# Two-layer gated attention: modulation rows computed in row form, first unit and last tiles reordered, and the second layer's norm bias folded in on GpSimd

## What is computed

```python
xn = _ln(x, ln_w, ln_b)
q = softmax(heads(xn @ Wq + bq), axis=channels of a head)
k = softmax(heads(xn @ Wk + bk + mask), axis=tokens)
v = (xn @ Wv + bv) * mask
att = einsum('bnhd,bnhl->bhdl', k, v)
y = einsum('bnhd,bhdl->bnhl', q, att)
scale, shift = split(silu(emb) @ W_emb + b_emb, 2)      # "film": one pair of rows for each sequence
hh = _ln(y, ln2_w, ln2_b) * (1.0 + scale) + shift
return x + silu(hh) @ W_out + b_out
```

## Time and profile before

| | |
|---|---|
| median of 3 runs | 791.82 us |
| lowest and highest | 791.3 and 793.96 us |
| the profiled execution's own time | 790.92 us |
| its span (first to last instruction) | 789.1 us |
| busy share PE, DVE, ACT, POOL | 96%, 88%, 66%, 56% |
| mean granted TensorE clock | 0.996 of full speed |
| chain of work that ended last | PE 78%, DVE 12%, ACT 4% |

### The profile page before, as it was taken

How to read it: one execution, slowest core, us unless ns; L and a number is a source line. 1 busy time by engine, 2 the same in 40 slices (tenths; PEclk the granted TensorE clock), 3 DMA queues, 4 the chain that set the end, 5 groups by cost and what they waited for, 6 DMA issues and landing times.

```text
span 789.1 us, 17594 instructions
## 1 busy us (share of the span) xinstructions
PE 760.7 (96%) x6719; PEld 405.7 (51%) x6719; DVE 693.9 (88%) x1427; ACT 517.4 (66%) x1011; POOL 439.3 (56%) x433
## 2 busy tenths in 40 slices
PE   5997999999999999999999999999999999999996
PEld 2446446464564545546464554646464554645442
DVE  7898979788998999999988899898888899888985
ACT  5896767666667687786866685665658476560733
POOL 2465583653836768487664755547265535637323
PEclk9998999999999999999999999999999999999999
DMA  9966896865949759596585939688594939578452
GB/s 325 311 132 168 271 183 192 161 145 150 185 139 161 189 129 182 170 173 189 109 188 138 195 108 184 165 161 201 93 203 120 187 122 178 130 140 156 83 132 81
DMA packets 291252, 130.78 MB, mean 166 GB/s; under 512 B 261440, under 2 KB 261824, under 8 KB 291168
## 3 DMA queue, kind: packets, MB, share of 16 engines
q1 hardware_dynamic: 288432, 125.27, 71.1%
q10 hardware_dynamic: 2736, 4.39, 1.6%
HBM read 47.74 MB, written 16.88 MB: 82 GB/s over the span
## 4 chain that ended last, share of the span: by engine, by line
PE 78%; DVE 12%; ACT 4%; issue 3%; DMA 2%; SPq 1%; POOL 0%; DVEq 0%; ACTq 0%; POOLq 0%
PE ring L534 59%; PE ring L583 5%; PE ring L589 3%; PE att_ps L682 3%; DVE sb_k_or_qt L1069 2%; PE ring L730 2%; PE ring L594 2%; DMA sb_k_or_qt<-sb_tanh 1%; ACT sb_k_or_qt L1467 1%; PE ring L738 1%; DVE sb_row_peak L908 1%; DVE sb_q_max L1102 1%; DVE ring L1099 1%; DVE sb_ht_parts L1185 1%; DVE ring L1104 1%
## 5 line engine op out<-in xcount | busy, mean ns | idle before, releaser
L534 PE MATMUL ring<-sb_w_hi,sb_xt_parts 128*128 128x512 f16 x1024 | 309.2, 379 | 0.0
L534 PE MATMUL ring<-sb_w_lo,sb_xt_parts 128*128 128x512 f16 x512 | 194.2, 379 | 0.0
L534 PEld LDWEIGHTS ring<-sb_w_hi,sb_xt_parts 128*128 128x128 f16 x1024 | 100.4, 98 | 126.0 <-issue 6.6
L534 PE MATMUL ring<-sb_w_hi,sb_ht_parts 128*128 128x512 f16 x512 | 155.9, 380 | 4.3 <-DVE sb_ht_parts L1303 1.4
L1725 POOL TENSOR_TENSOR sb_htok<-sb_ht_parts,sb_htok 128x512 f16<-128x512 f32 x60 | 75.0, 1271 | 127.8 <-ACT sb_htok L1500 127.8
L1741 POOL TENSOR_TENSOR sb_tanh<-sb_v_or_q,sb_kq_hi 128x512 f16<-128x512 f32 x64 | 74.0, 1157 | 87.6 <-ACT sb_kq_hi L1531 87.0
L534 PE MATMUL ring<-sb_w_lo,sb_ht_parts 128*128 128x512 f16 x256 | 97.1, 379 | 0.0
L1524 ACT ACTIVATE sb_v_or_q<-ring,sb_ln_one 128x512 f32<-128x512 f32 x64 | 43.9, 686 | 60.9 <-DVE ring L1104 60.8
L534 PEld LDWEIGHTS ring<-sb_w_hi,sb_ht_parts 128*128 128x128 f16 x512 | 50.1, 98 | 63.7 <-ACT sb_ht_parts L1637 4.1
L1716 POOL TENSOR_TENSOR sb_x<-sb_x,sb_bias_o 128x512 f32<-128x512 f32 x64 | 79.3, 1276 | 5.8 <-DVE sb_w_lo L985 5.8
L534 PEld LDWEIGHTS ring<-sb_w_lo,sb_xt_parts 128*128 128x128 f16 x512 | 50.1, 98 | 59.4 <-issue 0.7
(11 more groups left out here) (244 smaller groups left out, 1573.5 us busy)
## 6 DMA issues: line engine op xcount, KB each, us to landing
out<-sb_x SPq DMA_DIRECT2D x14, 1024.0 KB, 5.8
sb_rows_now<-film_rows SPq DMA_DIRECT2D x16, 512.0 KB, 4.8
sb_x<-out SPq DMA_DIRECT2D x8, 1024.0 KB, 5.3
sb_x<-in_x SPq DMA_DIRECT2D x7, 1024.0 KB, 5.5
sb_mask_add<-mask_terms SPq DMA_DIRECT2D x15, 256.0 KB, 6.1
sb_w_hi<-in_L_cond_W_emb SPq DMA_DIRECT2D x1, 1536.0 KB, 14.0
sb_w_lo<-in_L_cond_W_emb SPq DMA_DIRECT2D x1, 1536.0 KB, 14.3
sb_w_hi<-in_L_cond_film_emb_W ACTq DMA_DIRECT2D x1, 1536.0 KB, 11.7
```

What stands on the lines that cost most here:

```text
L534: last = nc.tensor.matmul(out, lhs, rhs, start=(n == 0), stop=(n == len(pairs) - 1))
```

## The change

- Film stays in rows. Channel groups of 128 lie in four groups of 32 partitions; b_emb comes in by matmuls; `turn_film`, `turn_table` and four ACT copies go. The second norm's weight and bias are turned into rows once at the start (`ln2_in_rows`, one ACT copy). The rows are stored by four DMAs in place of two, in unit 0 between two transposes of the SP queue.
- Unit 0: film products come after query tiles 0 and 2; DVE does `v_scales` ahead of query tile 2, mixes values with queries, and does `mask_attention` ahead of most sums; attention uses half-width matmuls; x sums and squares of unit 2 move behind. The output weight's peak goes to the end of unit 0 on DVE, its scale and split into unit 1: on ACT ahead of `high_values(1)`, on POOL ahead of `low_values(1)`, its sum on PE after value tile 0. Both halves of layer 1's film weight are loaded by ACT in unit 1.
- Units 3 to 5: `shift_parts` and its ACT copy go; POOL does it with four multiplications and three additions of 128x512 float32, between `low_x` and `low_h`, once the weight is loaded.
- Unit 15: ACT takes the scaled values out of PSUM in float32 and then as float16; POOL makes the low part, so that DVE has no values to do.
- Tail: ACT's Silu replaces tanh and DVE's gate; h's power of two goes into the split; transposes on PE go in between matmuls of the projections.

```diff
@@ sync @@
             def store_table(layer):
-                sp.wait_ge(table_copied, 2 * (layer + 1))
-                for n in range(2):
-                    sp.dma_start(film_d[layer, :, n, :], table[film_part[n], :]).then_inc(film_stored, 16)
+                sp.wait_ge(film_ready, layer + 1)
+                for c in range(C):
...
+                    sp.dma_start(out, film[rows:rows + B].rearrange("b n (j e) -> b n j e", j=2)).then_inc(film_stored, 16)
...
-                turn_x(0, 1)
+                turn_x(0, 1, (0,))
+                store_table(0)
+                turn_x(0, 1, (1,))
@@ tensor @@
             def film_product(layer, half):
...
+                for c in range(C):
+                    at = B_EMB + C * half + c
+                    nc.tensor.matmul(out[film_part[c], :], cols[:, layer, at:at + 1].broadcast_to([P, 32]), ident[:], start=True, stop=False)
                 for k in range(KE):
-                    g = slice(k % 4 * 32, k % 4 * 32 + 32)
-                    last = nc.tensor.matmul(film_at(half)[g, :], emb_wide[:, k, :], film_w_at(half, k), start=(k < 4), stop=(k >= 4))
+                    for c in range(C):
+                        last = nc.tensor.matmul(out[film_part[c], :], emb_wide[:, k, :], film_w_at(half, k)[:, c * P:c * P + P],
+                                                start=False, stop=(k == KE - 1))
                 last.then_inc(film_half, 1)
...
             def shift_sums(layer, m):
-                pe.wait_ge(shift_copied, folded(layer, m))
+                if layer:
+                    pe.wait_ge(shift_row, 4 * PREPARED[1].index(m) + 4)
+                else:
+                    pe.wait_ge(shift_copied, folded(layer, m))
...
-                project_tokens("V", 0, V_, xt_hi, xt_lo, between=with_v)
-                first_attention(between=lambda: turn_table(0))
-                pe.wait_ge(table_copied, 2)
-                sum_w(0, O_)
+                project_tokens("V", 0, V_, xt_hi, xt_lo)
+                bound_film(0)
+                first_attention()
                 attend(0)
...
-                    if shifted is not None and i == 0:
+                    if shifted is not None and i == 2:
                         pe.wait_ge(h_ready, 4 * u)
-                        shift_parts(1, shifted)
-                    elif shifted is not None and i == 2:
                         shift_sums(1, shifted)
...
+                def with_v(i):
+                    if u == 1 and i == 0:
+                        sum_w(0, O_)
...
-                output(u - 1, (2, 3))
+                output(u - 1, (2,))
+                output(u - 1, (3,), at=((2, lambda: turn_h(0)),))
...
-            turn_h(0)
             turn_h(1)
             last_output(0)
-            last_output(1)
-            turn_h(2)
-            last_output(2)
-            turn_h(3)
+            last_output(1, ((1, lambda: turn_h(2)),))
+            last_output(2, ((2, lambda: turn_h(3)),))
             last_output(3)
@@ vector @@
+            def rows_of_film(layer):
...
+                for n in range(2):
+                    link(nc.vector.scalar_tensor_tensor(out=film[:, n, :], in0=film_at(0), scalar=1.0, in1=ln2_rows[:, layer, n, :],
+                                                        op0=ALU.add, op1=ALU.mult))
+                link(nc.vector.tensor_tensor(film[:, 1, :], film_at(1), film[:, 1, :], ALU.add))
...
             def keys_beside_h(u):
...
+                if u == 1:
+                    find_scale(0, O_)
+                    output_scale(0)
...
                 queries(0, 1)
+                v_scales(0)
                 queries(0, 2)
+                values(0, 0)
                 queries(0, 3)
-                v_scales(0)
-                values(0, 0)
                 values(0, 1)
                 values(0, 2)
-                gather_film(0)
+                rows_of_film(0)
                 values(0, 3)
+                find_film_peak(0)
+                query_sums(0, (0,))
                 film_scales(0)
-                find_peak(0, O_)
-                query_sums(0)
-                query_recip(0)
                 dve.wait_ge(blocks_loaded, 16)
                 mask_attention(0)
-                find_scale(0, O_)
-                output_scale(0)
+                query_sums(0, (1, 2, 3))
+                query_recip(0)
                 attended_all(0)
+                find_peak(0, O_)
@@ scalar @@
+            def last_silu(t):
...
+                nc.scalar.activation(kt_or_y[:, t, :], kt_or_y[:, t, :], ACT.Silu, scale=z_down[:]).then_inc(h_ready, 1)
...
+                    if u == LAST:
+                        act.wait_ge(done["V"], 4 * u + t + 1)
+                        nc.scalar.activation(v_of(u)[:, t, :], bank("V", t, u), ACT.Copy, scale=scale_down[:, layer, V_:V_ + 1]
+                                             ).then_inc(v_full, 1)
+                        act.wait_ge(v_full, t + 1)
+                        nc.scalar.copy(v_hi[:, t, :], v_of(u)[:, t, :]).then_inc(v_hi_ready, 1)
...
                 h_beside_keys(u)
+                if u == 1:
+                    scale_and_split(0, O_)
                 high_values(u, range(T))
-                if prepares is not None:
-                    copy_shift(1, prepares)
...
+            act.wait_ge(ln2_turned, 1)
+            nc.scalar.copy(ln2_rows[:].rearrange("p l n e -> p (l n e)"), ring[5]).then_inc(ln2_ready, 1)
             split_high(K_)
@@ gpsimd @@
+            def shift_rows_of(m, u):
+
+                pool.wait_ge(w_loaded[m], 16 if m == K_ else 32)
+                pool.wait_ge(y_scaled, 4 * u)
+                pool.wait_ge(qt_lo_ready, 16 * u)
...
+                nc.gpsimd.tensor_scalar(shift_rows(1, m), stages[1][m][:, 0, :], cols[:, 1, LN_B:LN_B + 1], None, ALU.mult).then_inc(shift_row, 1)
+                for c in range(1, C):
...
+                    nc.gpsimd.tensor_scalar(tanh[:, c % 2], stages[1][m][:, c, :], cols[:, 1, LN_B + c:LN_B + c + 1], None, ALU.mult
+                                            ).then_inc(shift_term, 1)
...
+                    nc.gpsimd.tensor_tensor(shift_rows(1, m), shift_rows(1, m), tanh[:, c % 2], ALU.add).then_inc(shift_row, 1)
...
                 low_x(u + 1, 3)
+                if PREP <= u < PREP + 3:
+                    shift_rows_of(PREPARED[1][u - PREP], u)
                 low_h(u - 1)
+                if u == 1:
+                    low_weight(0, O_, o0_ready)
                 if layer_of(u) == 0:
                     low_values(u)
...
-                low_queries(u)
+                for t in range(T):
+                    low_queries(u, (t,))
+                    low_values(u, (t,))
                 low_attention(u)
```

More of the change, by code:

```diff
@@ L633, in bound_film @@
                 nc.tensor.matmul(sum_at(FILM), ones[:], peak[:, layer, FILM:FILM + 1], start=True, stop=True).then_inc(film_bounded, 1)
-            def turn_table(layer):
-                pe.wait_ge(film_ready, 2 * (layer + 1))
-                for n, table in enumerate((film_g, film_s)):
-                    for c in range(C):
-                        out = film_ps[film_part[n], :].rearrange("b (j c e) -> b c j e", j=2, c=C)[:, c]
-                        last = nc.tensor.matmul(out, table[:, c, :], ident[:], start=True, stop=True)
-                last.then_inc(table_turned, 1)
             def sum_w(layer, m):
@@ L1183, in gate @@
             def gate(unit, t):
+                assert unit != LAST
                 dve.wait_ge(tanh_ready, 4 * unit + t + 1)
@@ L1429, in unused, with x_sums @@
                 return hp_hi if unit <= 2 else v_hi
-            def x_sums(unit):
+            def x_sums(unit, tiles=range(T)):
                 act.wait_ge(x_loaded[unit % XR], 16 * (unit // XR + (unit % XR > 0)))
```

262 lines of the change are left out of this document (113 added, 149 removed).

## The result

The changed kernel takes **803.2 us** (median of 4 runs, 801.2 to 803.72) against 791.77 for the kernel before on the same chip: a ratio of 1.0134, 95% interval 1.0119 to 1.0149. I had predicted 789.8, in a range of 783.5 to 796.5. The profiled execution took 802.97 us, its span is 801.0 (before: 790.92 and 789.1).

The account below looks back on a forecast made before the run. PE was taken as the bound, busy 760.7 us of a 789.1 us span. Terms -4.0 +5.6 +1.6 -1.1 -1.5 -2.65 = -2.05, from the median before of 791.82, gave 789.8 us, range 783.5 to 796.5.

Parts of the forecast that it names:

- Unit 0: Start and first unit: Y starts at 67.6 instead of 71.56, -4.0 us.
- Unit 1: Output weight's split on ACT ahead of the values delays attention: +5.6 us, and +1.6 for a clock fall.
- The rival by which the split finds room: In unit 1 attention is not held by the output weight's split, so -4.0 stays: 782.6 us; chance 0.10.
- Unit 2: No film turning, and film products in four groups run side by side: -1.1 us.
- The rival film in rows: Film groups in unit 2 do not run side by side: +8 in place of -1.1, 798.9 us; chance 0.06.
- Units 3 and 4: PE sheds shift work, GpSimd rows cost DVE 2.5 us a unit: -2.4+0.6 and -1.0+0.5 us.
- Unit 5: GpSimd's rows end after the old start of its low part, values end 3.8 us late, attention starts late: +0.8 us.
- the bounds behind it: Units 3 to 5 together: from -4.4 us (GpSimd's work for nothing) to +4.5 (DVE waits, PE with it, one clock fall).
- the price of the port between DVE and GpSimd: Units 3 to 5, among the keys: a DVE instruction waits for one GpSimd instruction, 1.50 against 0.76 us; +2.5 us DVE each.
- The first rival: Units 3 to 5: GpSimd's seven instructions hold DVE's key work, values late, PE idles: +4.5 for -1.5, 795.8 us; chance 0.24.
- The rival of cheap GpSimd rows: Units 3 to 5: GpSimd's rows are cheap and fit its holes, -4.4 us, 786.9 us; chance 0.20.
- Last unit and tail: Y of unit 15 about +0.6 us later; tail alone -3.25 us through Silu and transposes between matmuls; together -2.65.

Follow-up runs that it names:

- experiment 3: Changed kernel with the output weight's peak, scale and split moved earlier and a GpSimd pause in unit 5; 788.45 us, ratio 0.9948.
- experiment 12: Changed kernel with the output weight prepared early and the second layer's norm bias times weights back on TensorE and ScalarE, no pause; 785.3 us, ratio 0.9907.
- experiment 1: Changed kernel plus one wait: in unit 5 GpSimd adds the output bias only after VectorE has scaled the query sums; 793.86 us, ratio 1.0023.
- experiment 5: Changed kernel with one tiny VectorE fill ahead of the scaling of the query sums in unit 5; 802.4 us.
- experiment 7: Changed kernel with the output weight's preparation moved early, without a GpSimd pause; 796.11 us, ratio 1.005.
- experiment 9: Changed kernel with unit 5's scaling of the query sums written as an instruction with two SBUF inputs; 803.66 us.
- experiment 6: Changed kernel with five tiny VectorE fills ahead of unit 5's query-sum scaling; five runs 802.9 to 804.3 us, three 793.58, 794.06 and 796.73.
- experiment 11: Kernel before the change with only the second layer's norm bias times weights moved to GpSimd; 795.81 us, ratio 1.0067.
- experiment 4: Kernel before the change with 2 to 18 tiny VectorE fills ahead of the query-sum scaling in units 6, 7 and 9 to 14; 793.09 us.
- experiment 8: Kernel before the change with 7, 9 and 12 tiny VectorE fills ahead of the query-sum scaling in units 4, 5 and 6; 792.7 us.
- experiment 10: Changed kernel with a GpSimd pause ahead of unit 5's low attention part and eight VectorE fills before the query-sum scaling; 795.1 us.

## Why the prediction was wrong

**Unit 0, right.** Y starts at 68.0 where I had 67.6; the masked attention of the earlier trace rows is no longer held by the peak. The attention ended at 66.6 where I had 66.3. PE's last wait there is for the low attention part, 1.41 us at 68.00.

**Unit 1, right,** mechanism and size: +6.9 for +7.2. Attention starts at 108.73 where I had 108.3, and waits for GpSimd's fourth low value; the split stands at 97.53, ahead of the values. Experiments 3 and 12 show by undoing it that this is the cause. The rival by which the split finds room is refuted.

**Unit 2, right:** -1.2 for -1.1. The four column groups run side by side: the half of the film product takes 1.49 us for 48 of its records and 2.2 us in all, and not 6.4. The rival film in rows is refuted.

**Units 3 and 4, the sign wrong by 3.2 us together** (+0.9 for -2.3). GpSimd's durations were nearly right: four products and three sums of 11.6 us in unit 5 where I had 10.9. What they cost DVE I had too high: 2.5 us in each unit, against 1.7, 1.7 and 1.2 us in units 3, 4 and 5, counted on the two groups of rows that I had named. Two affine rows (L1169) take 2.68 us in unit 3 and 2.67 in unit 4, where the kernel before has 1.41; the four `low_keys` (L1058) take 4.16 us in unit 3 in both kernels, 4.51 instead of 4.12 in unit 4 and 5.32 instead of 4.12 in unit 5; the rest is the first affine row of unit 3, 1.20 instead of 0.74. What I left out is who waits for DVE then. In rows 207.72 and 256.11 PE waits 2.23 and 1.07 us for the fold of the new bias (L950), an instruction of DVE's queue between the third and the fourth query. Before, it was in time. What TensorE no longer had to do became idle time ahead of that fold: in unit 3 it sheds 2.4 us, and attention starts only 0.4 us earlier after the first key than before; in unit 4 it sheds 1.0, and attention starts no earlier. In unit 3 the granted clock fell behind the wait, too (0.83 from 205 to 215 us). In experiment 1 the same wait of 2.23 us passed at a clock of 1.00, and unit 3 took 48.2 us, so the fall cost 1.5.

**Unit 5, the step that failed:** "+0.8" and the bounds behind it. I had GpSimd's values end 3.8 us late; counted from the start of the unit's keys they end 4.5 late (301.68 + 4.48 - 270.4 against 298.45 - 267.2), and attention starts 1.8 late instead of 0.8. That part had the right mechanism and was somewhat too small: without the long instruction (experiment 1) the unit costs +2.4. But the price of the port between DVE and GpSimd was taken as one GpSimd instruction for each DVE instruction (0.76 against 1.50 us), and only among the keys, where I looked for it. The first rival priced four of seven such waits and +4.5 us at most for three units. In the trace after one instruction waited for eight, 0.24 us of work became 9.30 us, and behind it stand the residuals and the weight's peak, for which PE waits in the middle of its queue. So the rival had the right pair of engines and a wrong place, and its price had no room for a run. It is also the reason why the range did not hold, since without the hold the kernel takes 793.9 us and lies inside it. No row before shows a wait for more than one instruction, so the hold could not be read from them; but my own sum had filled GpSimd's last hole (11 us of new work against 7.4), and I did not ask what a queue without one does to the DVE instructions beside it.

The Trainium skill, "SBUF — State Buffer", section "Who interferes with whom", says that the first to issue has the shared pair for its whole instruction and that the other blocks until it is done. Of the short waits that is what the traces show (up to 1.4 us, the longest at the seam of two GpSimd instructions); the held rows go beyond it, and there the measurement decides: the wait lasted eight GpSimd instructions.

The rival of cheap GpSimd rows is refuted: one product takes 1.56 to 2.01 us. The 769 ns of the Trainium skill, "GPSIMD Engine Reference", section 3.1, is below half of the shortest of these rows; they multiply by a column, which may or may not be what that figure is for.

**Last unit and tail, nearly right:** +1.5 up to Y of unit 15 and -3.4 behind it, for +0.6 and -3.25. In unit 15 attention still waits 1.0 us for the last low value.

**What stays open** is why GpSimd's queue holds DVE in some executions and not in others: by their times in every run of the changed kernel and of experiments 5, 7 and 9, in five of eight of experiment 6, in none or two of seven in experiment 11. The point within the first addition (held at 0.02 to 0.89 us, not held at 0.00 to 0.82 in experiments 4 and 8), the length of the run behind it (experiments 8 and 10) and the form of the DVE instruction (experiment 9) do not decide. That a GpSimd pause ahead of the run, perhaps one of 0.1 us, decides is what all the profiles agree with, but no run tests a pause that short.

## What to carry to other kernels

Work moved to an engine that is "only 56% busy" is paid at the place where its queue fills up: add up what the engine must do between two of its idle rows, not over the kernel, and where it has no hole left, let it wait for each short instruction of VectorE that others wait for. One such wait cost GpSimd 0.21 us and gave the kernel back some 9. When a reordering ends one stage 4 us early, look first at what it put ahead of the next stage's first consumer; here the split of one weight, moved into a hole of the same engine, decided between a gain of 0.9% and none.

## What the runs showed of the hardware that I had not expected

- A DVE instruction of 0.24 us with its operands in SBUF lasted 8.59 to 9.49 us in five profiles, beside GpSimd instructions of 128x512 that followed one another without a pause, and ended within 0.1 us of the last of them; by the times of the runs, the same program ran with and without it. With a GpSimd pause of 0.93 us shortly before, it took 0.94; where GpSimd waited for it before its run began, 0.52.
- GpSimd's multiplication of 128x512 float32 by a column takes 1.56 to 2.01 us in the twelve rows of the changed kernel, its addition of two tiles 1.27 in seven of nine rows and 1.56 in two.
- Float32 matmuls of 128x128 in four groups of 32 columns: 48 of them in 1.49 us.
